# Scan over tokens dealt to eight groups, with one step over spans of 8 and six steps of one matmul each; order of u, B u, residual and splits in the first slot

## What is computed

```python
proj = h @ W_in                                   # 256 -> 384 data, 384 gate
conv = sum((xp[:, j:j + seq, :] * conv_w[:, j] for j in range(K)))
u = jax.nn.silu(conv)
M = jnp.eye(S, dtype=x.dtype) + A.T               # S = 16
Bu = jnp.einsum('bti,si->tbs', u, Bm)
def step(state, bu_t):
    s = state @ M + bu_t
    return (s, s)
_, states = jax.lax.scan(step, init, Bu)
y = jnp.einsum('tbs,is->bti', states, Cm)
out = jax.nn.sigmoid(gate) * y @ W_out
```

## Time and profile before

| | |
|---|---|
| median of 3 runs | 1416.96 us (1415.2 to 1417.71) |
| the profiled execution's own time | 1418.72 us |
| its span, first to last instruction | 1416.8 us |
| mean granted TensorE clock | 0.989 |
| PE busy | 1373.8 us, 97% |
| DVE busy | 1153.7 us, 81% |

### The profile page before, as it was taken

The page is one execution under the profiler, slowest core; times in us unless marked ns, Lnnn a source line. Parts: engine busy times, 40 slices in busy tenths (PEclk is TensorE's granted clock), DMA queues, the critical chain, the costliest instruction groups (busy, mean ns, idle before and its releaser), DMA issues. The chain is left out here.

```text
span 1416.8 us, 21192 instructions
## 1 busy us (share of the span) xinstructions
PE 1373.8 (97%) x7050; PEld 1220.9 (86%) x7050; DVE 1153.7 (81%) x2192; ACT 675.7 (48%) x1347; POOL 706.2 (50%) x636
## 2 busy tenths in 40 slices
PE   6989999999999999999999899999999999999997
PEld 5879999999999999999999777878787878878776
DVE  7887786777858768686678698989898999999866
ACT  5611402103022130130101398888888888888983
POOL 2421301313013121130123287888888888989897
PEclk9989999999999999999999899999999999999999
DMA  9101011100111001100138410000001000000000
GB/s 264 42 15 29 20 38 37 31 27 27 40 31 40 28 27 40 31 25 23 53 105 267 148 61 16 16 30 16 31 10 37 8 23 23 16 31 16 10 14 30
DMA packets 83133, 62.96 MB, mean 44 GB/s; under 512 B 13984, under 2 KB 75856, under 8 KB 82768
## 3 DMA queue, kind: packets, MB, share of 16 engines
q1 hardware_dynamic: 54880, 45.94, 10.3%
q10 hardware_dynamic: 28144, 15.67, 3.7%
HBM read 36.55 MB, written 25.03 MB: 43 GB/s over the span
## 5 line engine op out<-in xcount | busy, mean ns | idle before, releaser
L1741 PE MATMUL ps<-w_hi,memory_r 128*128 128x384 f32 x2048 | 565.5, 342 | 0.0
L1442 DVE SCALAR_TENSOR_TENSOR wst<-ps,w_cur,wst 128x384 f32<-128x384 f32 x480 | 295.1, 615 | 164.4 <-PE ps L1741 152.4
L1962 POOL TENSOR_TENSOR memory_rest<-memory_rest,pf 128x512 f32<-128x512 f32 x248 | 345.8, 1394 | 68.5 <-ACT pf L2069 60.4
L1741 PEld LDWEIGHTS ps<-w_hi,memory_r 128*128 128x128 f32 x2048 | 374.9, 189 | 3.4 <-issue 1.4
L1741 PE MATMUL ps<-w_lo,memory_r 128*128 128x384 f32 x1024 | 344.0, 336 | 0.0
L2135 DVE TENSOR_TENSOR p_lo<-pf,p_hi 128x512 fp32r<-128x512 f32 x256 | 282.1, 1102 | 36.0 <-ACT p_hi L2071 35.0
L1741 PEld LDWEIGHTS ps<-w_lo,memory_r 128*128 128x128 f32 x1024 | 193.3, 189 | 4.7 <-issue 1.4
L2069 ACT ACTIVATE pf<-ps 128x512 f32<-128x512 f32 x256 | 153.1, 598 | 72.8 <-PE ps L2241 54.8
L2029 ACT COPY ps<-shift_rows 128x512 f32<-128x512 f32 x254 | 151.7, 597 | 5.8
L2071 ACT ACTIVATE p_hi<-ps 128x512 fp32r<-128x512 f32 x256 | 152.1, 594 | 0.0
L2116 DVE TENSOR_REDUCE mx<-ps 128x1 f32<-128x512 f32 x224 | 147.6, 678 | 1.2 <-PE ps L2230 1.2
(11 more groups left out here) (256 smaller groups left out, 2211.2 us busy)
## 6 DMA issues: line engine op xcount, KB each, us to landing
qk_scratch<-wst ACTq DMA_DIRECT2D x56, 128.0 KB, 2.2
x_scratch<-memory SPq DMA_DIRECT2D x8, 512.0 KB, 2.9
o_scratch<-memory_rest SPq DMA_DIRECT2D x16, 256.0 KB, 3.2
x2b<-x_scratch SPq DMA_DIRECT2D x32, 128.0 KB, 2.2
out_x<-memory_rest SPq DMA_DIRECT2D x32, 128.0 KB, 1.7
v_scratch<-wst ACTq DMA_DIRECT2D x60, 64.0 KB, 1.8
memory<-in_x SPq DMA_DIRECT2D x7, 512.0 KB, 4.0
memory_r<-qk_scratch SPq DMA_DIRECT2D x9, 256.0 KB, 4.6
```

Of the source, the lines that this page charges most:

```text
L1442: nc.vector.scalar_tensor_tensor(out=dst, in0=src, scalar=w, in1=dst, op0=ALU.mult, op1=ALU.add).then_inc(moe_acc, 1)
L1741: ins = nc.tensor.matmul(ps[:, s % MOE_BANKS, 0:H3], x_part[p][:, k, rows], w_part[:, k, e].rearrange("p t h -> p (t h)"), start=(k == 0 a ...
L1962: nc.gpsimd.tensor_tensor(p_sum[:, p], p_sum[:, p], pf[:, j % PB], ALU.add).then_inc(p_summed, 1)
```

## The change

**Tokens are dealt.** Group g now holds the tokens 8 n + g, n = 0 to 63. A token 8 or more earlier, at a distance of 8 times a power of two, is then always in the same group, some columns to the left. The steps for distances 8, 16, ... 256 (six of them) take one matmul each, and add in place to the columns from d on. The seven distances 1 to 7 are taken together in a first step, of two matmuls that accumulate: `near[:, 0]` for partners in the same column, `near[:, 1]` for those in the column before. `SCAN` goes from 9 to 7.

**The near matrices.** `strip` holds M^0 to M^7, 16 by 16 each, from small matmuls and copies beside the first powers; 8 DMAs spread it over the diagonals of `near`. They are issued on SP behind the loads of experts 3 to 9, wait there for `pow_ready` 4, and those of experts 10 to 15 stand behind them. The scan's first matmul waits for all 8 (`a_in`).

**The layout is undone by access patterns.** The sigmoid (ACT) and the product (POOL, in the first two blocks DVE) read `cv` with a step of 8 numbers (32 bytes) and write `sg` in a row. `gate_times_y` reads y in PSUM with a step of 64 numbers.

**The first slot and the prologue are reordered.** B u of block (0, 1) moves from steps 1 to 3 to step 3 in one piece. Its convolution, sigmoid and u are cut into three (f = 0, 1, 2): u of f = 0 and 1 is made ahead of the route, u of f = 2 behind it. Of the splits on DVE, 2 to 4 leave the scan's steps and 6, 7 the place ahead of gate times y: 2 is made behind the scan, 3 and 4 by POOL, 5 ahead of the convolution, 6 and 7 behind u, 8 to 15 at steps 5 to 12. POOL's residual of block (0, 1) waits for split 7 and stands ahead of `xt_lo`. The first `norm` piece of slot (0, 0) stands at relative step 4 in place of 2.

```diff
@@ the scan
+    POWERS = BT.bit_length() - 1
+    SCAN = POWERS - 2
...
+                for g in range(NB):
+                    sp.dma_start(near[g * S:(g + 1) * S].rearrange("p l n -> p (l n)")[:, (g + 1) * S:(g + NB) * S],
+                                 strip[:, 1:NB].rearrange("p n s -> p (n s)")).then_inc(a_in, 16)
...
-                    src, dst = scan_s[k % 2], ps[:, SCAN_BANK0 if first else X0, (k % 2) * GT:(k % 2 + 1) * GT]
-                    if d < GT:
-                        nc.tensor.matmul(dst[:, d:GT], pw_m(k), src[:, 0:GT - d], start=True, stop=True)
-                        ins = nc.tensor.matmul(dst[:, 0:d], pw_m(k, 1), src[:, GT - d:GT], start=True, stop=True)
-                    else:
-                        ins = nc.tensor.matmul(dst, pw_m(k, d // GT), src[:], start=True, stop=True)
+                    src, dst = scan_s[1 if k else 0], ps[:, SCAN_BANK0 if first else X0, (k % 2) * GT:(k % 2 + 1) * GT]
+                    if k:
+                        d = (1 << k) // 2
+                        ins = nc.tensor.matmul(dst[:, d:], powers[:, k + 2], src[:, 0:GT - d], start=True, stop=True)
+                    else:
+                        nc.tensor.matmul(dst, near[:, 0], src[:], start=True, stop=False)
+                        ins = nc.tensor.matmul(dst[:, 1:], near[:, 1], src[:, 0:GT - 1], start=False, stop=True)
@@ the layout
+        def by_group(a):
+            return a.rearrange("p f (n g) -> p f g n", g=NB)
+        def grouped(a):
+            return a.rearrange("p f (g n) -> p f g n", g=NB)
...
-                    nc.gpsimd.tensor_tensor(sg, sg, cv, ALU.mult).then_inc(u_ready, 1)
+                    nc.gpsimd.tensor_tensor(grouped(sg), grouped(sg), by_group(cv), ALU.mult).then_inc(u_ready, 1)
...
-                    nc.scalar.activation(sg, cv, ACT.Sigmoid).then_inc(csig_ready, 1)
+                    nc.scalar.activation(grouped(sg), by_group(cv), ACT.Sigmoid).then_inc(csig_ready, 1)
...
-                    tt(gy, gy, ps[:, X0:X0 + FI, :], ALU.mult).then_inc(gy_ready, 1)
+                    y = gy.rearrange("p f (n g) -> p f n g", g=NB)
+                    tt(y, y, ps[:, X0:X0 + FI, :].rearrange("p f (g n) -> p f n g", g=NB), ALU.mult).then_inc(gy_ready, 1)
@@ the strip, on PE and on the copying engine
+                    if k in (2, 3):
+                        n = 1 << (k - 1)
+                        ins = nc.tensor.matmul(ps[0:S, QK_BANK, 2 * P:2 * P + n * S], mt[0:S, 0:S],
+                                               strip[:, 0:n].rearrange("p n s -> p (n s)"), start=True, stop=True)
@@ the first slot
-        LATE_SPLIT, FIRST_BU = 8, 1
+        POOL_SPLIT, LATE_SPLIT, SPLIT_AHEAD, FIRST_BU = 3, 8, 3, 3
...
-                        if is_first(i, p) and LATE_SPLIT + s < E:
-                            split_w(LATE_SPLIT + s, LATE_SPLIT + s + 1)
+                        if is_first(i, p) and LATE_SPLIT <= s + SPLIT_AHEAD < E:
+                            split_w(s + SPLIT_AHEAD, s + SPLIT_AHEAD + 1)
```

More of the change, by code:

```diff
@@ L683, in _ @@
                                       b_wide[:, P:P + FI * P].rearrange("p (f n) -> p f n", n=P)[:, :, 0:S])
+                pool.wait_ge(w_lo_ready, POOL_SPLIT)
+                for n in range(POOL_SPLIT, POOL_SPLIT + 2):
+                    pool.wait_ge(w_hi_ready, n + 1)
+                    nc.gpsimd.tensor_tensor(w_lo[:, :, n], w_raw[:, :, n], w_hi[:, :, n].bitcast(F32), ALU.subtract
+                                            ).then_inc(w_lo_ready, 1)
                 low_hidden(0, 1)
@@ L1388, in _ @@
                    ).then_inc(dve_const, 1)
+                split_w(2, POOL_SPLIT)
                 norm_piece(4, 0, 1)
```

159 lines of the change are left out of this document (90 added, 69 removed).

## The result

The changed kernel takes 1407.6 us (median of 4 runs, 1404.81 to 1410.01) against 1416.7 in the same comparison: a ratio of 0.9937, 95% interval 0.9919 to 0.9955, 9 us less. The profiled execution of before is 1.8 us above its median, that of after (1404.81 us, span 1403.0, clock 0.997) is the fastest of its four. So the two traces differ by 13.9 us and the medians by 9, and I read the difference place by place, not from the ends.

A forecast was written before the change was run, and what follows sets the result against it. PE's own instructions bound the later slots; DVE paces the first scan and, after the change, slot (0, 0). Later slots -9, prologue and slot (0, 0) -10.5, access patterns +3.5: -16 us, 1401 against 1417; range 1394.5 to 1410.

The forecast's parts named there:

- one engine at twice: Only ACT's or POOL's strided reads take twice as long: -8 to -13 us, 1404 to 1409; 0.18 shared with the clock.
- two signs of being wrong: PE's waits for low parts or `wst` in steps 8 to 16 far from 6 us; 32-byte step costing more than half.
- The later slots, -9: Scan steps in the six slots behind the first: 3.4 us of PE becomes 1.9, so 1.5 us a scan.
- The prologue, -2.7: First scan 3.4 us shorter, its start about 0.6 us later: 2.7 us gained; strided accesses there cost 1.5 us, counted separately.
- Slot (0, 0), -7.8 of its own: Slot (0, 0) leaves with 10.5 us gained, the prologue's 2.7 in it; new PE waits take about 6 us.
- DVE's account: DVE in slot (0, 0): accumulations begin at 78.9 in place of 80.70, backlog gone at 111.4 in place of 118.98.
- The access patterns, +3.5: Strided reads 15 to 20 per cent longer: slack covers later slots, 1.5 us in the prologue, 2 for DVE's late accumulations.
- The near matrices at nothing: The 8 DMAs land at 34.5 us, PE wants them at about 37.5: 3 us of slack, no cost.
- It costs less: Strided reads are free and DVE catches up sooner: -19.5 to -23 us, 1394 to 1397.5; chance 0.13.
- All strided reads at twice: Strided reads take twice as long, 18 + 3 us in place of 3.5: -5 to +2, 1412 to 1419; chance 0.08.
- The clock falls again in slot (0, 0): New PE waits lower the clock for ten steps, some 5 us: -11, 1406; 0.18 shared with one engine at twice.
- Slower: u late at B u in six slots, if sigmoid and product take 2.3 times their 4.4 us; chance 0.05.

The follow-up runs named there:

- the second profile: The changed kernel profiled again with no edit: 1407.18 us median of 6 runs, ratio 0.9929 to the kernel before; its profiled execution took 1408.4 us.

## Why the prediction was right, and where its sizes were off

1407.6 lies in the range, 6.6 us above the forecast of 1401 and outside the forecast's own 1397.5 to 1405: 9 us came of 16. It is in the range that was given 0.18 (one engine at twice, or the clock again). The mechanism held: the slots' stream shortened, the wait of 5.44 us went, and with it the low clock in the first profile, and new waits for DVE took back about half of slot (0, 0). Of its own two signs of being wrong, one came: the step of 32 bytes costs more than half, on each of the three engines. The other came in part: the waits for low parts and `wst` are 3.6 us and not 6, and the scan's 2.3 and some short ones make up the sum.

Place by place the first trace has 11.9 of the 16 us; the 2.9 from there to the 9 of the medians are the spread of the executions. Three terms were too large.

- **The later slots, -9.** Measured -6.2. The two-matmul and one-matmul steps cost what was read (0.36 and 0.15 us). So did the 0.09 us counted for the matmul that follows (0.26 us for 0.17): with it the pieces take 3.4 us before and 1.9 after, as was summed. Yet the period fell by 1.23 us without the step of 32 bytes and not by 1.5. The missing 0.27 us is spread over the expert matmuls, and no run shows why. A further 0.2 went to the step, at B u: 1.03 with it. Over six slots these two are the 2.8 us.
- **The prologue, -2.7 and 1.5 against it for strided accesses.** The run without a step has 2.5 us of the 2.7. With it, 0.4 to 0.8 are left: the strided accesses cost 1.7 to 2.1 here. Inside the term, the scan was shortened by 3.3 us as counted, and the start of it came later by 1.3 us even without the step, where 0.6 was put; two profiles of one kernel differ by 1.2 us at this place, so its parts are rough. Not counted was the wait of 1.4 us behind POOL's splits, costed at nothing because they "lie where it was idle": idle was POOL, but DVE wasn't.
- **Slot (0, 0), -7.8 of its own.** Measured -5.3, and -4.2 in the second profile. The new waits were sized rightly in sum, 6.4 us of idle time for "about 6", and the run without late splits confirms the reason that was given for them. The gross was too large. Clock and scan were to take 5.8 + 1.5 = 7.3 us off PE's busy time, and took 5.2. The run without late splits, with hardly a wait, has 104.26 - 97.51 = 6.8: so 0.5 us was counted too much, and 1.5 us of busy time are the price of the new waits, which was not in the sum.
- **DVE's account** (accumulations from 78.9, backlog gone at 111.4): 82.16 and 117.78. The start is late by the strided u, 0.4 us three times, and by the prologue's loss; without a step it was 79.15. The end is late because the splits are not the only work that ran beside POOL: the copy to `w_all` took 1.84 us, too; in the run without a step that wait of DVE stands at 115.66, so the late start is part of it.
- **The access patterns, +3.5.** They cost 3.2 us in the medians (1404.2 against 1407.4), near the number, and by luck: 1.5 was to be in the prologue and 2 in DVE's lateness, and 2 were in the prologue and 1.2 in the later slots. 15 to 20 per cent was wrong: the step makes ACT's read 2.07 times as long (1.50 to 3.11), DVE's 1.6, POOL's 1.52. What hid it was more than the slack of 2.1 us that was counted: a further 1.0 us lay between the sigmoid's end at 250.99 and the product's start at 252.00, where POOL was not free yet. The two use 3.1 us more (1.6 and 1.5), and 2.1 + 1.0 is 3.1; the rest is the 0.1 to 0.2 us by which B u is late. By the rule of the Trainium skill, page "GPSIMD Engine Reference" ("Performance pitfalls for Q7 kernels"), POOL was to go up by half: the rows agree, 4.42 against 2.91. The page "SBUF — State Buffer" names the penalty for leaving a line of 16 bytes with each access, without a figure; the rows supply two.
- **The near matrices at nothing**: right, with about 5.6 us of slack instead of 3.

**The rivals.** "It costs less" fell: with no step at all the kernel takes 1404.2. "All strided reads at twice" named its 21 us from two terms that did not come: POOL's is half more and gate times y had none, and the slack held for nearly all of the rest. Its smaller case, one engine at twice, names the range that was measured (1404 to 1409), and ACT did read at twice; but it was priced at 6.5 to 11.5 us, and the steps cost 3.2, so the match is chance.

"The clock falls again in slot (0, 0)" came in part. Of the eleven profiles with the new order of this slot (the changed kernel's two and nine of the experiments), three have a granted clock of 1.00 over it and eight 0.95 to 0.98; before it was 0.94. It cost less than the 5 us of the rival: in these eight the slot takes 104.7 to 106.6 us, in the changed kernel's first profile 105.43. The run without a step has 0.97, more busy time of PE than the changed kernel's first profile at 1.00, less idle time, and the same length:

```profile
70.63:176.06 105.43, 101.05 (x566) 94.78 (x565) 83.32 (x194) 20.64 (x40) 26.85 (x19) 0.97 0.10 29
```

Where DVE sets the pace, a slower PE waits less. That reading is argued from these windows; no run sets the clock.

"Slower" needed 2.3 times for sigmoid and product together (its 10.3 us are 2.34 times): they take 1.7 times (7.54 us), and that is already a little beyond the point from which every further tenth is paid in each slot.

## What to carry to other kernels

Moving an instruction to an idle engine is free only if the engine that it runs beside is idle too, or runs instructions then that are not held (below: accumulations from PSUM, statistics): look at the pair, not at the engine. And a pattern that undoes a layout belongs on the engine and the side where it costs nothing: read all rows of before for such a step first, and where there are none, put the step where the slack is larger than a doubling. Where two edits are worth 3 us each and a median is known to 1.3, ask the places in the traces whether they add up, and not the medians.

## What the runs showed of the hardware

- **DVE stands still beside POOL**, for some kinds of instruction. Five places above: a modulation of 0.51 us took 1.70, a copy 1.84 (0.18 elsewhere), a convolution of two instructions 4.52 (1.54), splits 1.28 and 2.07 (0.95), and each ended, behind POOL's instruction, within the time that it takes alone. The accumulations, whose one input is PSUM, kept their 0.60 to 0.62 us in the same stretch. Working on SBUF alone is not enough for it. Two rows of DVE of the changed kernel, beside a POOL instruction that ran from 36.30 to 38.66:

```profile
36.08 1.40 DVE L1023 BATCH_NORM_STATS2 bst<-memory 128x6 f32<-128x256 f32 x4
...
37.92 1.56 DVE L1018 TENSOR_TENSOR w_lo<-w_raw,w_hi 128x768 fp32r<-128x768 f32 x1
```

  The statistics, which read one tensor from SBUF, took 0.41 us each as everywhere; the split behind them, which reads two, took 1.56 for 0.95. The page "SBUF — State Buffer" of the Trainium skill ("Who interferes with whom") says it: with two inputs in SBUF, or in a copy's faster mode, DVE and POOL lock each other out, and the second waits for the whole instruction of the first. The rows agree, but for one kind: beside POOL's reciprocal root of 4 numbers (41.92 to 43.08 by the profile) two modulations kept their 0.48 us. There the measurement decides.
- **A step in SBUF has a price by engine and side.** For 32 bit numbers, in us in a row and with the step: ACT reading with 32 bytes 1.50 and 3.11; POOL reading one of two inputs 2.91 and 4.42, writing with 256 bytes 3.01; DVE 0.69, reading 1.13, writing with 256 bytes 1.08. DVE reading PSUM with 256 bytes: 1.755 either way.
- **The clock costs what waits leave.** Two windows of before: PE stands still from 75.5 to 80.93, and the granted clock falls within that wait and stays at the lower level (0.50, 1.2 GHz) for 11.8 us of work behind it:

```profile
75.49:79.10 3.61, 0.01 (x1) 0.00 (x0) 3.06 (x15) 0.57 (x2) 0.00 (x0) 1.00 0.00 0
...
80.93:92.70 11.77, 11.77 (x50) 11.77 (x50) 9.41 (x8) 0.00 (x0) 7.71 (x3) 0.50 0.17 45
```

  With waits of up to 1.8 us in this slot it was 1.00 over the slot in one execution and 0.98 in another of the same kernel.
